# A descriptor ring of 32 KB, scans that write over their gathered rows, and two scans at other places in the order

## The chip, the core and the metric

The kernel runs on one core of a Trainium2 chip. The metric is the device time of one launch in microseconds (us). A core has five engines with queues of their own: PE (matrix products), DVE (vector work and scans along a row), ACT (functions by table), POOL (here: indirect DMAs, which gather or scatter rows by a list of indices) and SP (here: all other DMAs). Engines wait for one another and for DMAs by semaphores. An indirect DMA is prepared by POOL itself: it writes descriptors, one for each row to be moved, into a ring in on-chip memory, from which 16 DMA engines take them.

## What is computed

A vision tower on 16 images of 56 x 56 positions with 64 channels: a gated 3 x 3 token stage, a class token put ahead of each image, a layer norm with a linear recurrence along the sequence, and a mixture of four experts whose gates come from graph attention. The part that the change touches is the graph attention, over 16,384 nodes and 262,144 edges:

```python
h = (x_flat @ W_gat).reshape(M, HEADS, NUM_EXPERTS)
a_src = (h * att_src).sum(-1); a_dst = (h * att_dst).sum(-1)
e = leaky_relu(a_src[src] + a_dst[dst], negative_slope=0.2)
e_max = segment_max(e, dst)
ee = exp(e - e_max[dst])
alpha = ee / (segment_sum(ee, dst)[dst] + 1e-16)
agg = segment_sum(h[src] * alpha[:, :, None], dst) + b_gat
```

## The kernel before

**Front.** Two lanes of 56 steps go through the token stage, the recurrence and the projection, in 64 turns (`TURNS`); each engine works on a different step in one turn. The steps write the table of node rows (24 floats: h, a_src, a_dst) to HBM. Beside turns 4 to 22 the edges are sorted by destination on DVE, PE and ACT, POOL searches the first edge of each node (L766, 128 gathers of 128 indices each) and scatters a_dst to the first edges (L773, 128 scatters; the last 10 come after the gathers of chunk 0).

**Gathers.** The edges lie sorted as 128 rows (partitions) of 2048 columns. POOL then gathers the source rows from the table, one column at a time: L796 runs 2048 times, each time 128 rows of 24 floats. They go in 17 chunks k: fifteen of 128 columns, one of 96, one of 32. Chunk k lands in `ring[k % 2]`, a tile in on-chip memory (not the descriptor ring). Every run of 128 has semaphores of its own, two that take turns in groups of four; ahead of each group POOL waits until the group two before it has landed (`gather_group`, L753).

**Scans.** When chunk k has landed, DVE runs scan k (L1606): a running maximum, and running sums of the weights and of the weighted rows, along each partition. It reads `ring[k % 2]` and writes into `res[k % 2]`; SP stores that to `partial` in HBM and loads the a_dst of chunk k+2 (`scan_moves`, L554). POOL begins chunk k >= 2 when scan k-2 is done (`scan_used`, L793); scan k waits for the store of chunk k-2 (L1649).

**Order.** All orders are written out by hand. `SCAN_AFTER_TURN` puts scans 0 to 6 behind turns of the front, on DVE, ACT (its exponentials) and SP (its store) alike; `SCAN_AFTER_PAIR` puts scans 7 to 11 behind pairs of 512-node expert blocks, which follow the front; the others come after the last pair.

**Tail.** After the last store POOL joins the segments across partitions (L800, L803) and gathers the last edge row of each node (L811, 128 gathers); DVE, ACT and PE mix the experts' outputs and the result is stored. Ahead of that SP loads the table rows of the nodes themselves into the free half of `ring` (L657).

Of the kernel before, what the change touches and what calls it, by code (L numbers as in the profile page):

```python
# [5 lines left out]
i32 = mybir.dt.int32  # L6
bf16 = mybir.dt.bfloat16
# [26 lines left out]
P = 128  # L34
# [58 lines left out]
SC = 128  # L93
# [31 lines left out]
SCAN_AFTER_TURN = {31: 0, 37: 1, 43: 2, 49: 3, 55: 4, 61: 5, 63: 6}  # L125
# [21 lines left out]
def build(nc, x, cls_tok, tokW1, tokb1, tokW2, tokb2, tokW3, tokb3, A_diag, Bmat, Cmat, Dvec, dtv,  # L147
# [12 lines left out]
    with ctx:  # L160
# [48 lines left out]
        ring_all = sb("ring", [P, 2 * SC * TW])  # L209
        ring = [ring_all[:, n * SC * TW:(n + 1) * SC * TW].rearrange("p (a b) -> p a b", b=TW) for n in range(2)]  # L210
        res = [sb(f"res{n}", [P, SC, RW]) for n in range(2)]
        raw = [sb(f"raw{n}", [P, SC, HEADS]) for n in range(2)]
        ad = sb("ad", [P, HEADS, SC])
        e = sb("e", [P, HEADS, SC])
        mx = sb("mx", [P, HEADS, SC + 1])
# [19 lines left out]
        keys = [t[:, :, :].rearrange("p a b -> p (a b)")[:, 0:COLS] for t in res]  # L235
        dst_in = ns[:, :].bitcast(i32)
        dst_i = ring_all[:, 2 * COLS:3 * COLS].bitcast(i32)
        dst_f = keys[0]
        own_a = res[0][:, :, :].rearrange("p a b -> p (a b)")[:, COLS:COLS + P * HEADS].rearrange("p (a b) -> p a b", b=HEADS)
# [3 lines left out]
        iota_wide = ring_all[:, 2 * COLS:2 * COLS + SB * P // 2].bitcast(bf16).rearrange("p (a b) -> p a b", b=SB)  # L243
# [189 lines left out]
        def _(sp):  # L433
# [120 lines left out]
            def scan_moves(k):  # L554

                sp.wait_ge(S["scan_used"], k + 1)
                d(partial_v[:, FROM[k] * RW:(FROM[k] + SIZES[k]) * RW],
                  res[k % 2][:, 0:SIZES[k], :].rearrange("p a b -> p (a b)")).then_inc(res_st[k % 2], 16)
                if k + 2 < SCHUNKS:
                    load_raw(k + 2)  # L560
# [94 lines left out]
            for k in range(max(SCAN_AFTER_PAIR.values()) + 1, SCHUNKS - 1):  # L655
                scan_moves(k)
            d(own.rearrange("p (m j) w -> p m (j w)", j=FF), table[0:GRAPH_NODES, :]  # L657
# [20 lines left out]
        def _(pool):  # L678
# [106 lines left out]
            for k in range(SCHUNKS):  # L785
# [6 lines left out]
                if k >= 2:  # L792
                    pool.wait_ge(S["scan_used"], k - 1)  # L793
# [469 lines left out]
        def _(dve):  # L1263
# [342 lines left out]
            def scan(k):  # L1606
# [6 lines left out]
                ov = res[q][:, 0:n, :].rearrange("p c w -> p w c")  # L1613
# [35 lines left out]
                wait(dve, res_st[q], 16 * (k // 2))  # L1649
                v.tensor_copy(ov[:, 0:HEADS, :], mx_k)  # L1650
                for h in range(HEADS):
                    v.tensor_tensor_scan(ov[:, HEADS + h, :], old[:, h, :], new[:, h, :],
                                         car[:, HEADS + h:HEADS + h + 1], ALU.mult, ALU.add)
                    for x_ in range(EXPERTS):
                        w = h * EXPERTS + x_
                        v.tensor_tensor_scan(ov[:, 2 * HEADS + w, :], old[:, h, :], msg_k[:, w, :],
                                             car[:, 2 * HEADS + w:2 * HEADS + w + 1], ALU.mult, ALU.add)
                v.drain()
                v.tensor_copy(car[:, :], res[q][:, n - 1, :])
# [331 lines left out]
```

## Time and profile before

| | us |
|---|---|
| time, median of three runs (3934.3 to 3937.07) | 3935.76 |
| the profiled execution's own time | 3940.46 |
| its span, first to last instruction | 3938.5 |
| POOL busy | 2467.8 (63%) |
| DVE busy | 2236.6 (57%) |
| PE busy | 1959.2 (50%) |
| ACT busy | 1172.2 (30%) |
| gathers of L796: busy, idle ahead of them | 2023.7, 661.2 |

Shares of busy time are means over stages with different limits. To read them, take the stage apart in which one engine works without a break, and look at what ends each of its gaps. "issue" as the end of a gap says that the profile shows nothing that the engine waited for. The time of a POOL row for an indirect DMA is that of preparing it, not of moving the data.

### The profile page before, as it was taken

Reading aid. Unit: us, or ns where it says so; the run is one execution under the profiler, and the core shown is the slowest. Engines: PE = TensorE matmul, PEld = TensorE weight load, DVE = VectorE, ACT = ScalarE, POOL = GpSimd, SP = SyncE. Lnnn points to the kernel's source line nnn. Section 1 sums busy time; section 2 is a strip of 40 time slices with the busy share of each in tenths; the row PEclk is TensorE's granted clock in tenths of the full one; section 3 lists DMA queues with packets and bytes.
Section 4 is the critical chain, followed back from the end, with each engine's and each line's share of the span. In section 5 each row is a group of like instructions: output and inputs, shape, how many; then the busy total and the mean of one; then the engine's idle time right before and its main releaser. Section 6 shows DMA issues by size and latency. Waiting matters only on the chain. (4 is left out here: it accounts for less than half of the span.)

```text
span 3938.5 us, 28658 instructions
## 1 busy us (share of the span) xinstructions
PE 1959.2 (50%) x7633; PEld 850.9 (22%) x7633; DVE 2236.6 (57%) x3952; ACT 1172.2 (30%) x1736; POOL 2467.8 (63%) x2477
## 2 busy tenths in 40 slices
PE   0441119998876868686865036785863300000034
PEld 0111113333222323232322012332321100000023
DVE  8889987887567666767677555544322020210355
ACT  0120005554543434343433024553553300000000
POOL 1000007776777777777777777777777777777573
PEclk9975558998987989897977568997987755555567
DMA  4110004543443434444431433232332310111133
GB/s 110 26 26 0 0 11 76 100 77 69 76 70 77 78 73 75 83 71 77 81 60 27 78 51 78 67 86 69 86 112 52 111 28 10 28 10 27 39 116 127
DMA packets 651925, 247.81 MB, mean 63 GB/s; under 512 B 552260, under 2 KB 632564, under 8 KB 649332
## 3 DMA queue, kind: packets, MB, share of 16 engines
q1 hardware_dynamic: 573844, 216.69, 23.4%
q0 software_dynamic: 77920, 29.29, 7.2%
q8 instruction: 62, 1.02, 0.1%
q14 instruction: 99, 0.81, 0.1%
HBM read 152.62 MB, written 91.71 MB: 62 GB/s over the span
## 5 line engine op out<-in xcount | busy, mean ns | idle before, releaser
L796 POOL DMA_INDIRECT ring<-table,src_i x2048 | 2023.7, 988 | 661.2 <-issue 546.9
L766 POOL DMA_INDIRECT ring<-keys_d,place x128 | 147.7, 1154 | 627.6 <-DVEq L1269 587.5
L1625 DVE TENSOR_TENSOR_SCAN ad<-ns,cad,raw 128x128 f32<-128x128 f32 (+2 forms) x68 | 26.5, 451 | 745.6 <-DMA ring<-table,src_i 745.5
L1003 PE MATMUL ps<-arena 64*128 64x512 f32 x800 | 219.2, 670 | 396.8 <-DMA arena<-xnT 259.7
L898 PE MATMUL ps<-arena,w 64*128 64x448 f32 x896 | 255.4, 650 | 185.8 <-DVE arena L1668 114.6
L1050 PE MATMUL ps<-ident,ends 128*20 128x128 f32 x6 | 1.5, 414 | 596.3 <-DVEq L1865 596.3
L1123 ACT ACTIVATE ex<-ex 128x1024 f32<-128x1024 f32 (+2 forms) x17 | 17.1, 1006 | 831.0 <-DVE ex L1640 831.0
L1200 ACT ACTIVATE arena<-ps,arena 128x1024 f32<-128x1024 f32 x200 | 213.0, 1115 | 116.9 <-PE ps L1003 116.8
L1668 DVE TENSOR_TENSOR arena<-arena,ps 128x448 f32<-128x448 f32 x297 | 172.1, 616 | 115.5 <-ACT ps L1117 115.3
L911 PE MATMUL ps<-arena,w 128*64 128x448 f32 x896 | 216.5, 606 | 39.3 <-issue 39.3
L1117 ACT ACTIVATE ps<-ps,tb 128x448 f32<-128x448 f32 x297 | 169.6, 605 | 210.1 <-PE ps L898 190.2
L1682 DVE TENSOR_TENSOR_SCAN arena<-ps,carry,arena 128x448 f32<-128x448 f32 x122 | 130.7, 1131 | 163.2 <-ACT arena L1166 163.1
L1312 DVE TENSOR_TENSOR res<-res 128x512 f32<-128x512 f32 (+1 forms) x259 | 208.0, 803 | 13.2
L1836 DVE TENSOR_TENSOR arena<-ps,arena 128x1024 f32<-128x1024 f32 x68 | 83.3, 1225 | 221.1 <-PE ps L1025 220.6
L1313 DVE TENSOR_TENSOR res<-res 128x512 f32<-128x512 f32 (+1 forms) x259 | 206.5, 797 | 0.0
L1014 PE MATMUL ps<-arena 128*64 128x512 f32 x800 | 194.1, 606 | 0.0
L1003 PEld LDWEIGHTS ps<-arena 64*128 64x128 f32 x800 | 74.3, 201 | 534.4 <-issue 238.0
L888 PE MATMUL ps<-arena,w 128*64 128x448 f32 x896 | 186.6, 559 | 0.0
L773 POOL DMA_INDIRECT adst_d<-res,place x128 | 147.3, 1151 | 62.5 <-issue 38.2
L853 PE MATMUL ps<-ident,res 128*128 128x128 f32 x224 | 54.0, 422 | 243.2 <-DVE res L1335 193.2
L1207 ACT ACTIVATE arena<-ps,arena 128x512 f32<-128x512 f32 x200 | 126.6, 684 | 140.1 <-PE ps L1014 139.7
L1117 ACT ACTIVATE arena<-ps,tb 128x448 f32<-128x448 f32 x207 | 121.5, 631 | 128.9 <-PE ps L898 101.0
(346 smaller groups left out, 3952.1 us busy)
## 6 DMA issues: line engine op xcount, KB each, us to landing
arena<-in_x SPq DMA_DIRECT2D x304, 110.0 KB
ring<-table,src_i POOLq DMA_INDIRECT x2048
partial<-res SPq DMA_DIRECT2D x15, 1536.0 KB, 6.1
arena<-in_x SPq DMA_DIRECT2D x160, 140.0 KB
outputs_d<-arena SPq DMA_DIRECT2D x32, 512.0 KB, 2.8
arena<-outputs_d SPq DMA_DIRECT2D x32, 512.0 KB, 4.9
arena<-xnT SPq DMA_DIRECT2D x100, 128.0 KB, 3.1
arena<-h_tok SPq DMA_DIRECT2D x50, 256.0 KB
```

Of the source, the lines that this page charges most:

```text
L766: g.indirect_dma_start(out=blocks[:, k, :], out_offset=None, in_=keys_d[:, :], in_offset=off(ap=place[:, k:k + 1], axis=0)).then_inc(done, 16)
L796: g.indirect_dma_start(out=ring[k % 2][:, j - FROM[k], :], out_offset=None, in_=table[0:GRAPH_NODES, :], in_offset=off(ap=src_i[:, j:j + 1 ...
L888: mm(o[lower_upper(z), :], w1[:, i, :], tap_view(s, 2 * i + z), start=i == 0, stop=False, skip_group_check=True)
L898: mm(bank(1 + (2 * i + z) % 3)[:, 0:CHUNK], w2[lower_upper(z), i * P:(i + 1) * P], h1[lower_upper(z), :], start=True, stop=True).then_inc( ...
L911: mm(bank(4)[lower_upper(z), 0:CHUNK], w3[:, i, :], prod[:, 2 * i + z, :], start=i == 0, stop=False, skip_group_check=True)
L1003: m = mm(hid[ee % 2][:, z * NT:(z + 1) * NT], fw1[lower_upper(z), ee, :], xf[q][lower_upper(z), :], start=True, stop=True)
L1014: m = mm(sy[lower_upper(h), t * NT:(t + 1) * NT], fw2[:, ee, :], hh[k % 2][:, z, ee, :], start=True, stop=True)
L1117: a(gate_of(s, t), bank(1 + t % 3)[:, 0:CHUNK], ACT.Sigmoid, bias=tb2[:, t // 2:t // 2 + 1])\
L1200: a(hh[k % 2][:, :, ee, :], hid[ee % 2].rearrange("p (z n) -> p z n", z=2), ACT.Gelu, bias=fb1[:, ee:ee + 1]).then_inc(S["hh_done"], 1)
L1312: v.tensor_tensor(d4[:, :, 0:halves], low, high2, ALU.min)
L1313: v.tensor_tensor(d4[:, :, halves:size], high, low2, ALU.max)
L1668: v.tensor_tensor(r3(prod[:, t, :]), tap_view(s, t), r3(gate_of(s, t)), ALU.mult)\
```

## The change

1. The descriptor ring that POOL fills for its indirect DMAs has 32 KB in each partition, not 16 (`dynamic_dma_scratch_size`).
2. The tiles `res` are gone, which makes room for it. Scan k writes its results over the rows that it has read, in `ring[k % 2]`, and the store reads them there. The sort's key tiles, which lay in `res`, lie in an enlarged `ring`; some short-lived tiles moved into one new tile, `early_i`.
3. POOL therefore begins chunk k >= 2 when the store of chunk k-2 has landed (`res_st`), not when scan k-2 is done. Scan k no longer waits for a store. SP waits for the store of chunk 15 before it loads the nodes' own rows over that half.
4. Scan 4 stands behind turn 54, not 55, and scan 5 behind turn 59, not 61.

```diff
--- before.py
+++ after.py
@@ -122,7 +122,7 @@
 RAW_AT = 26
 PSUM_FROM = GRAPH_STEPS + 4
 EARLY_STEPS = 17
-SCAN_AFTER_TURN = {31: 0, 37: 1, 43: 2, 49: 3, 55: 4, 61: 5, 63: 6}
+SCAN_AFTER_TURN = {31: 0, 37: 1, 43: 2, 49: 3, 54: 4, 59: 5, 63: 6}
 SCAN_AFTER_PAIR = {4: 7, 14: 8, 24: 9, 35: 10, 44: 11}
 GROUP = 4
 
@@ -206,13 +206,15 @@
         ns = sb("ns", [P, COLS])
         src_i = sb("src_i", [P, COLS], i32)
 
-        ring_all = sb("ring", [P, 2 * SC * TW])
+        ring_all = sb("ring", [P, 2 * SC * TW + COLS])
         ring = [ring_all[:, n * SC * TW:(n + 1) * SC * TW].rearrange("p (a b) -> p a b", b=TW) for n in range(2)]
-        res = [sb(f"res{n}", [P, SC, RW]) for n in range(2)]
-        raw = [sb(f"raw{n}", [P, SC, HEADS]) for n in range(2)]
-        ad = sb("ad", [P, HEADS, SC])
+        assert RW == TW
+        HW = HEADS * SC
+        early_i = sb("early_i", [P, 3 * HW + HEADS * (SC + 1)])
+        raw = [early_i[:, n * HW:(n + 1) * HW].rearrange("p (a b) -> p a b", b=HEADS) for n in range(2)]
+        ad = early_i[:, 2 * HW:3 * HW].rearrange("p (a b) -> p a b", a=HEADS)
+        mx = early_i[:, 3 * HW:3 * HW + HEADS * (SC + 1)].rearrange("p (a b) -> p a b", a=HEADS)
         e = sb("e", [P, HEADS, SC])
-        mx = sb("mx", [P, HEADS, SC + 1])
         ex = sb("ex", [P, 2, HEADS, SC])
         msg = sb("msg", [P, HE, SC])
         nb = sb("nb", [P, SC])
@@ -232,15 +234,15 @@
         fixed = sb("fixed", [P, RW])
         none = sb("none", [1, RW])
 
-        keys = [t[:, :, :].rearrange("p a b -> p (a b)")[:, 0:COLS] for t in res]
+        keys = [ring_all[:, (2 + n) * COLS:(3 + n) * COLS] for n in range(2)]
         dst_in = ns[:, :].bitcast(i32)
-        dst_i = ring_all[:, 2 * COLS:3 * COLS].bitcast(i32)
+        dst_i = early_i[:, 0:COLS].bitcast(i32)
         dst_f = keys[0]
-        own_a = res[0][:, :, :].rearrange("p a b -> p (a b)")[:, COLS:COLS + P * HEADS].rearrange("p (a b) -> p a b", b=HEADS)
+        own_a = e[:, :, :].rearrange("p a b -> p (a b)").rearrange("p (a b) -> p a b", b=HEADS)
         SB = SAMPLES // 4
         oh = [[ring_all[:, n * SB * P // 2:(n + 1) * SB * P // 2].bitcast(bf16)
                .rearrange("p (a b) -> p a b", b=SB) for n in (2 * q, 2 * q + 1)] for q in range(2)]
-        iota_wide = ring_all[:, 2 * COLS:2 * COLS + SB * P // 2].bitcast(bf16).rearrange("p (a b) -> p a b", b=SB)
+        iota_wide = ex[:, :, :, :].rearrange("p z a b -> p (z a b)").bitcast(bf16).rearrange("p (a b) -> p a b", b=SB)
         blocks = ring_all[:, 0:P * SAMPLE].rearrange("p (a b) -> p a b", b=SAMPLE)
         rowbase = sb("rowbase", [P, 1])
 
@@ -555,7 +557,7 @@
 
                 sp.wait_ge(S["scan_used"], k + 1)
                 d(partial_v[:, FROM[k] * RW:(FROM[k] + SIZES[k]) * RW],
-                  res[k % 2][:, 0:SIZES[k], :].rearrange("p a b -> p (a b)")).then_inc(res_st[k % 2], 16)
+                  ring[k % 2][:, 0:SIZES[k], :].rearrange("p a b -> p (a b)")).then_inc(res_st[k % 2], 16)
                 if k + 2 < SCHUNKS:
                     load_raw(k + 2)
 
@@ -654,6 +656,7 @@
                 load_y(hidx)
             for k in range(max(SCAN_AFTER_PAIR.values()) + 1, SCHUNKS - 1):
                 scan_moves(k)
+            sp.wait_ge(res_st[1 - last_ring], 16 * len(SIZES[1 - last_ring::2]))
             d(own.rearrange("p (m j) w -> p m (j w)", j=FF), table[0:GRAPH_NODES, :]
               .rearrange("(m p j) w -> p m (j w)", p=P, j=FF)).then_inc(S["rows_in"], 16)
 
@@ -790,7 +793,7 @@
                             scatter(tile_k, group_landed(scattered, n))
                             n += 1
                 if k >= 2:
-                    pool.wait_ge(S["scan_used"], k - 1)
+                    pool.wait_ge(res_st[k % 2], 16 * (k // 2))
                 for j in range(FROM[k], FROM[k] + SIZES[k]):
                     done = gather_group(k, j - FROM[k])
                     g.indirect_dma_start(out=ring[k % 2][:, j - FROM[k], :], out_offset=None, in_=table[0:GRAPH_NODES, :],
@@ -1610,7 +1613,6 @@
                     dve.wait_ge(done, gathered(k) // 2)
                 dve.wait_ge(raws[q], 16 * (k // 2 + 1))
                 rv = ring[q][:, 0:n, :].rearrange("p c w -> p w c")
-                ov = res[q][:, 0:n, :].rearrange("p c w -> p w c")
                 cs = slice(FROM[k], FROM[k] + n)
 
                 flag = ns[:, cs].unsqueeze(1).broadcast_to([P, HEADS, n])
@@ -1646,17 +1648,16 @@
                                     new[:, h, :].unsqueeze(1).broadcast_to([P, EXPERTS, n]), ALU.mult)
                 v.drain()
 
-                wait(dve, res_st[q], 16 * (k // 2))
-                v.tensor_copy(ov[:, 0:HEADS, :], mx_k)
+                v.tensor_copy(rv[:, 0:HEADS, :], mx_k)
                 for h in range(HEADS):
-                    v.tensor_tensor_scan(ov[:, HEADS + h, :], old[:, h, :], new[:, h, :],
+                    v.tensor_tensor_scan(rv[:, HEADS + h, :], old[:, h, :], new[:, h, :],
                                          car[:, HEADS + h:HEADS + h + 1], ALU.mult, ALU.add)
                     for x_ in range(EXPERTS):
                         w = h * EXPERTS + x_
-                        v.tensor_tensor_scan(ov[:, 2 * HEADS + w, :], old[:, h, :], msg_k[:, w, :],
+                        v.tensor_tensor_scan(rv[:, 2 * HEADS + w, :], old[:, h, :], msg_k[:, w, :],
                                              car[:, 2 * HEADS + w:2 * HEADS + w + 1], ALU.mult, ALU.add)
                 v.drain()
-                v.tensor_copy(car[:, :], res[q][:, n - 1, :])
+                v.tensor_copy(car[:, :], ring[q][:, n - 1, :])
                 v.drain()
                 v.nop().then_inc(S["scan_used"], 1)
 
@@ -1981,7 +1982,8 @@
         "b1": np.ascontiguousarray(g["L0_ffn_b1"].T), "W2": g["L0_ffn_W2"], "b2": row(g["L0_ffn_b2"]),
         "edges": g["L0_ffn_edge_index"],
     }
-    nc = bacc.Bacc("TRN2", target_bir_lowering=False, num_devices=1)
+    nc = bacc.Bacc("TRN2", target_bir_lowering=False, num_devices=1,
+                   dynamic_dma_scratch_size=32768)
     args = [nc.dram_tensor("in_" + k, a.shape, mybir.dt.from_np(a.dtype), kind="ExternalInput").ap()
             for k, a in arrays.items()]
     args.append(nc.dram_tensor("out", [NODES, CH], f32, kind="ExternalOutput").ap())
```

How this moves instructions is seen at two places. The first is DVE at the front's end, just ahead of scan 6 (whose first row here is L1625, or L1627 in the changed kernel). `ad` and `early_i` are the a_dst along the columns, `carry` is the state of the recurrence. Before:

```order
L1656 SCALAR_TENSOR_TENSOR res<-ex,car,msg 128x128 x4
L1659 COPY car<-res 128x24
L1718 SCALAR_TENSOR_TENSOR arena<-arena,d_sb,ps 128x448
L1721 TENSOR_TENSOR arena<-arena 128x448
L1748 TENSOR_TENSOR arena<-ps,arena 128x448
L1625 SCALAR_TENSOR_TENSOR ad<-ns,cad,raw 128x128 x4
L1626 TENSOR_SCALAR nb<-ns 128x128
L1627 COPY mx<-car 128x4
```

The same place in the changed kernel:

```order
L1765 TENSOR_TENSOR arena<-arena 128x448 x2
L1769 COPY carry<-arena 128x1 x2
L1719 SCALAR_TENSOR_TENSOR arena<-arena,d_sb,ps 128x448
L1722 TENSOR_TENSOR arena<-arena 128x448
L1749 TENSOR_TENSOR arena<-ps,arena 128x448
L1627 SCALAR_TENSOR_TENSOR early_i<-ns,cad,early_i 128x128 x4
L1628 TENSOR_SCALAR nb<-ns 128x128
L1629 COPY early_i<-car 128x4
```

The end of scan 5 (the rows that write `car`) is no longer ahead of scan 6: it went in front of turns 60 and 61, and the end of turn 61 (`carry`) stands there now.

The second is SP at the end, where it stores the last chunks and loads the nodes' own rows (`ring<-table`). In brackets is what an issue waits for. Before:

```order
L552 DMA raw<-adst_d 128x384
L557 DMA partial<-res 128x3072 [waits scan_used]
L552 DMA raw<-adst_d 128x128
L557 DMA partial<-res 128x2304 [waits scan_used]
L657 DMA ring<-table 128x32x96
L557 DMA partial<-res 128x768 [waits scan_used]
```

In the changed kernel:

```order
L554 DMA early_i<-adst_d 128x384
L559 DMA partial<-ring 128x3072 [waits scan_used]
L554 DMA early_i<-adst_d 128x128
L559 DMA partial<-ring 128x2304 [waits scan_used]
L660 DMA ring<-table 128x32x96 [waits res_st1]
L559 DMA partial<-ring 128x768 [waits scan_used]
```

The order is the same; the load now waits for the store ahead of it.

## Rows read from the trace of the kernel before

**Rows 1.** Busy time by stretch: L796 alone; then all engines, PE to POOL.

```profile
990.90:3688.40 2697.50, 2023.70 (x2048) 0.76 0.32 64
...
3688.40:3938.50 250.10, 85.41 (x330) 69.23 (x330) 121.34 (x282) 20.44 (x56) 135.74 (x130) 0.68 0.33 99
```

**Rows 2.** Groups by line: busy, mean ns, idle ahead, and its releasers.

```profile
L796 POOL DMA_INDIRECT ring<-table,src_i x2048 | 2023.7, 988 | 661.2 <-issue 546.9 <-DMA ring<-table,src_i 114.3
```

**Rows 3.** Waits of POOL: total us, times, longest us; whole run, then chunk 15.

```profile
POOL ring L796 <- issue: 546.9, 1697, 3.2
POOL ring L796 <- DMA ring<-table,src_i: 114.3, 351, 2.1
...
POOL ring L796 <- issue: 22.5, 74, 0.3
```

**Rows 4.** Timeline of POOL at three pauses: start, us, gather [idle before it].

```profile
1140.56 0.94 POOL L796 DMA_INDIRECT ring<-table,src_i  x1 [3.13 <-issue]
...
3171.57 0.94 POOL L796 DMA_INDIRECT ring<-table,src_i  x1 [0.30 <-issue]
3174.49 0.94 POOL L796 DMA_INDIRECT ring<-table,src_i  x1 [1.97 <-issue]
...
3503.78 0.94 POOL L796 DMA_INDIRECT ring<-table,src_i  x1 [2.01 <-issue]
```

**Rows 5.** Gathers from the first of chunks 0 and 12 to its pause.

```profile
L796 POOL DMA_INDIRECT ring<-table,src_i x113 | 112.3, 994 | 34.4 <-issue 29.9 <-DMA ring<-table,src_i 4.6
...
L796 POOL DMA_INDIRECT ring<-table,src_i x113 | 110.1, 974 | 34.9 <-issue 27.9 <-DMA ring<-table,src_i 7.0
```

**Rows 6.** Timeline: the start of scan 12 on DVE, and a gather beside it.

```profile
3194.43 1.61 DVE L1625 TENSOR_TENSOR_SCAN ad<-ns,cad,raw 128x128 f32<-128x128 f32 x4 [141.93 <-DMA ring<-table,src_i]
...
3204.00 2.01 POOL L796 DMA_INDIRECT ring<-table,src_i  x1 [0.30 <-issue]
```

**Rows 7.** SP issues the stores of chunks 3, 4, 5; landing of all 17.

```profile
1810.44 0.33 SPq L557 DMA_DIRECT2D partial<-res  x1
...
2001.24 0.32 SPq L557 DMA_DIRECT2D partial<-res  x1
...
2170.12 0.32 SPq L557 DMA_DIRECT2D partial<-res  x1
...
DMA to landing us min/median/max: 2.3/6.1/6.6
```

**Rows 8.** The first gathers of chunks 5, 6 and 7.

```profile
1845.91 0.94 POOL L796 DMA_INDIRECT ring<-table,src_i  x1 [0.30 <-issue]
...
2015.04 0.94 POOL L796 DMA_INDIRECT ring<-table,src_i  x1 [0.30 <-issue]
...
2183.56 0.94 POOL L796 DMA_INDIRECT ring<-table,src_i  x1 [0.30 <-issue]
```

**Rows 9.** DVE: ends of turns 54 and 59; starts of scans 4, 5, 6.

```profile
1950.17 0.21 DVE L1768 COPY carry<-arena 128x1 f32<-128x1 f32 x2
...
1977.57 1.61 DVE L1625 TENSOR_TENSOR_SCAN ad<-ns,cad,raw 128x128 f32<-128x128 f32 x4
...
2111.29 0.21 DVE L1768 COPY carry<-arena 128x1 f32<-128x1 f32 x2
...
2146.45 1.61 DVE L1625 TENSOR_TENSOR_SCAN ad<-ns,cad,raw 128x128 f32<-128x128 f32 x4
...
2185.02 1.61 DVE L1625 TENSOR_TENSOR_SCAN ad<-ns,cad,raw 128x128 f32<-128x128 f32 x4 [6.99 <-DMA ring<-table,src_i]
```

**Rows 10.** The load of own rows on SP, and its first reader on DVE.

```profile
L657 SPq DMA_DIRECT2D ring<-table x1: 773/773/773, 3666.7 to 3666.7; - x1
DMA to landing us min/median/max: 11.7/11.7/11.7
...
3709.91 0.69 DVE L1905 TENSOR_TENSOR arena<-ring 128x512 f32<-128x512 f32 x1
```

**Rows 11.** DVE waits for the last search reads.

```profile
790.71 0.69 DVE L1559 TENSOR_TENSOR ring<-ring,msg 128x512 f32<-128x512 f32 x1 [1.05 <-DMA ring<-keys_d,place]
```

## The prediction

> **What bounds the kernel now.** I read first the busy time by stretch. All 2048 gathers of L796 lie in one stretch of 2697.5 us out of 3938.5; what follows is a tail of 250.1 us that works on their result [rows 1]. Within the stretch POOL is busy for 2023.7 us and idle for 661.2 us in gaps so short that no other engine can be blamed: 1697 gaps count as "issue" and 351 as waits for a gather's landing [rows 2, 3]. So the end of the program is the start of chunk 0 (991 us), plus 2048 gathers one behind the other, plus the tail; DVE does not hold POOL anywhere in it, and a scan is waited for only at the very end. A change is worth what it takes from POOL's row of gathers.
>
> Then I looked for gaps that are not like the others. An ordinary gap is 0.30 us. Chunk 15, which is 96 gathers, has 74 issue gaps of 22.5 us in total, 0.304 us each, the longest 0.3 [rows 3]. Over the whole loop the longest is 3.2 us [rows 3], and the timeline shows where the long ones lie: one in each of chunks 0 to 14, 15 in all, between 1.78 and 3.19 us; the first (3.13), that of chunk 12 (1.97) and the last (2.01) are shown [rows 4]. Their sum is 33.5 us, and 33.5 - 15 x 0.304 = **28.9 us** is more than ordinary gaps would take. The total agrees: 546.9 - 1697 x 0.304 = 31.0 us of issue time above the ordinary, so some 2 us lie elsewhere.
>
> The place of the pause is what matters. In chunk 0 and in chunk 12 alike, 113 gathers go out from the chunk's first one and the pause stands ahead of the 114th [rows 5]; the other 13 are 128 gathers apart. Between chunks 0 and 1 POOL also issues ten scatters, and the pause of chunk 1 is still ahead of the 114th gather of its chunk. So something fills up that is empty again at the start of each run of 128, and holds 113 DMAs. Chunks 15 and 16 have fewer than 113 columns and show no such pause. That is the size that the change doubles, as I read it: twice 113 is 226, and no run is longer than 128.
>
> **The change part by part.**
>
> The ring. 15 pauses go, if the count of 113 is the ring's: -28.9 us on POOL's row, at full price, since the next gather waits for nothing else there. What could be late next is the group wait ahead of every fourth gather; its 351 gaps are 114.3 us in total, 0.33 us each [rows 3], so groups have mostly landed by then, and I add nothing. The search and the scatters have a pause at their 114th DMA too, of about 1.4 us above the ordinary each. The scatter's is hidden: the step behind it waits for the front. The search's is waited for by DVE, 1.05 us [rows 11], and the front that sets the start of chunk 0 is behind DVE; between 0 and 1.05, and I take -1 us since nothing else is late there.
>
> Stores in place of scans, as what opens a chunk. POOL begins chunk k+2 at the landing of store k. A store lands 6.1 us after its issue, 6.6 at most [rows 7]. Without pauses (28.9 / 15 = 1.93 us each, and 1 us from the search) chunk 5 would start at 1845.9 - 5 x 1.93 - 1 = 1835.2 [rows 8]; store 3 goes out at 1810.4 [rows 7] and is down by 1817.0: 18 us of cover. Chunk 6 would start at 2015.0 - 12.6 = 2002.4; store 4 goes out at 2001.2 and, left where it is, would be down by 2007.8, 5 us late. Chunk 7 would start at 2183.6 - 14.5 = 2169.1; store 5 (2170.1 + 6.6 = 2176.7) would be 8 us late. Later scans start soon after their chunk has landed (scan 12 as shown [rows 6]) and take 23.7 us (scan 4: 1977.6 to its store at 2001.2 [rows 7, 9]), while the next chunk of 128 takes some 165: over 100 us of cover, and 98 for the chunk of 96. Price with the moves: 0. Behind the waiting gather on POOL there are only more gathers; nobody else waits for them before the chunk is full.
>
> The moves. Turn 55 lasts from 1950.2 to 1977.6 on DVE, so scan 4 and its store come 27.3 us sooner; turns 60 and 61 last from 2111.3 to 2146.5, so scan 5 comes 35 us sooner [rows 9]. Store 4 is then down by 1980, 22 us ahead of chunk 6; store 5 by 2142, 27 us ahead of chunk 7. Both scans find their chunk landed: the next chunks began at 1845.9 and 2015.0 [rows 8]. On SP the store and the load of a_dst for the chunk after next move along, past the x loads and step stores of one and two turns, and SP stands at the same wait for the scan, only sooner; the front's work of turns 55, 60 and 61 runs up to a scan's length (23.7 us) later, and nothing on POOL waits for it. Scan 6 waited 7.0 us for its chunk [rows 9] and still does, about 14 us sooner, and the expert pairs start as much sooner. Price: 0.
>
> Writing over the gathered rows. The operations of a scan keep their number, shape and stride (24 floats, in `res` as in `ring`); the one wait that goes (for a store two chunks back) had long been met. The nearest rows are those same instructions, so 0 either way; the sort's keys in another tile likewise.
>
> The nodes' own rows. Their load now starts when store 15 is down, about 4.6 us later than it did; it takes 11.7 us from 3666.7, and DVE reads it at 3709.9 [rows 10]. 31.5 us of cover less 4.6: 27 us. Behind it on SP is only the last store, which waits for scan 16. It no longer shares the DMA engines with store 15; the longest wait of a gather for a landing is 2.1 us [rows 3], so -1 to +2 us, and I take 0.
>
> Sum: -28.9 - 1 = about -30 us. The tail begins as much sooner and is unchanged. Made against the profiled execution: 3938.5 - 30 = 3908.5 of span; with 2 us around it 3910.5, against 3940.5. The median of the timed runs is 4.7 us below the profiled one, so 3935.8 - 30 = **3906 us**.
>
> **The rivals.**
>
> A, fewer pauses but not none. If the count runs on through the runs, one comes every 226 gathers: 2048 / 226 = 9 stay, 9 x 1.93 = 17.4 us, and the gain is 28.9 - 17.4 + 1 = 12.5: 3923. Against it: ten scatters between chunks 0 and 1 did not shift the place, and the later pauses lie 128 apart, not 113. The Trainium skill gives this case its mechanism: by "DMA: Bandwidth & Descriptors" (Terms, and The descriptor swizzle) a descriptor is 16 bytes and 128 rows make nine of them on each DMA engine, and by "SBUF — State Buffer" (SBUF size) the ring has 16 KiB per partition; an estimate from these pages is 1024 / 9 = 113.8 DMAs per round of the ring, wherever a run begins. The trace agrees with the 113 and not with rounds that run on.
>
> B, nothing, because the pause isn't the ring's. A mechanism of that kind is at work here: a gather beside scan 12 took 2.01 us to prepare where 0.94 is ordinary [rows 6], so DVE's work does slow POOL. If it also made the pauses, the ring would change nothing: 3935. Against it: at 3172.5 to 3174.5 DVE has been idle since scan 11, for 141.9 us up to scan 12 [rows 6], and the pause is there as in the other chunks. The Trainium skill has this as a rule: "SBUF — State Buffer", SBUF: two separate sides, says that POOL cannot write descriptors while DVE holds a port that they share. By that rule the time would stay at 3935; the trace agrees on the slowed gathers and not on the pauses.
>
> C, slower: POOL held at the stores. Place: the starts of chunks 5, 6 and 7, where the front is closest behind. The covers are 18, 22 and 27 us; it decides from there, if the front in its new order (or slower scans in place) runs that much later against the gathers, and each us more costs one. To lose on the whole it must eat the 30 us gained and 8 more, so a front some 60 us late by then, and a time above 3944. For it: without the moves two of the three would have been late. Against it: the front has the same work, of which a scan is 23.7 us.
>
> D, more than that: group waits and slowed gathers give up a little as well; 3897 at the best.
>
> **How the numbers follow.** Forecast 0.77, A 0.08, B 0.07, C 0.05, D 0.03. About 0.2% (8 us) is what a measurement can tell from no change. Faster by more: 0.77 + 0.08 + 0.03 = 0.88; within: B, 0.07; slower: C, 0.05. The forecast alone spans 3900 to 3912 (the unknown 0 to 1 of the search, -1 to +2 at the own rows, and gathers that fall otherwise beside DVE's work, some us either way). The range takes in A and most of D: 3898 to 3924, and leaves out B and C, 0.12, and a little of D.
>
> **What would show it.** In the profile after: no issue gap of L796 over 1 us; issue time about 517 us; last gather ending near 3658, the tail again 250 us. No wait of POOL for a `partial` store at a chunk's start (C shows there). Store 4 issued near 1973, store 5 near 2135. Pauses ahead of other gathers, at 226 or so, say A; at the 114th still, B. Wrong altogether I would be if the pauses only moved to the chunk starts.

## The result, and the profile after

The changed kernel takes **3911.0 us** (median of 6 runs, 3902.1 to 3913.4) against 3937.1 of the kernel before beside it (6 runs): a ratio of **0.9929, 95% interval 0.9916 to 0.9941**, 26 us less. The forecast was 3906, 30 us less, in a range of 3898 to 3924. The profiled execution took 3913.4 us, 27.1 us less than that of before; its span is 3911.4.

Busy time by stretch in the changed kernel (start:end, length, busy us of PE, PEld, DVE, ACT and POOL with their instruction counts, granted clock, DMA share, GB/s): up to the first gather, the gathers, the tail. It answers to [rows 1].

```profile
0.00:990.60 990.60, 502.89 (x1901) 224.71 (x1903) 839.53 (x1394) 276.23 (x440) 298.16 (x290) 0.78 0.26 50
990.60:3659.70 2669.10, 1368.56 (x5404) 554.05 (x5400) 1276.47 (x2278) 874.02 (x1240) 2027.13 (x2058) 0.76 0.33 65
3659.70:3911.40 251.70, 86.36 (x330) 69.91 (x330) 121.53 (x282) 20.40 (x56) 136.42 (x130) 0.68 0.33 98
```

The gather stretch is 28.3 us shorter (2669.1 against 2697.4 from first start to last end), it begins 0.5 us sooner, and the tail is 1.6 us longer, inside the 249.6 to 252.3 us that the tail took in the twelve kernels below. Then the gathers by line, and what POOL waited for (total us, times, longest us), as in [rows 2, 3]:

```profile
L799 POOL DMA_INDIRECT ring<-table,src_i x2048 | 2017.4, 985 | 639.2 <-issue 525.7 <-DMA ring<-table,src_i 113.6
```

```profile
POOL ring L799 <- issue: 525.7, 1706, 1.8
POOL ring L799 <- DMA ring<-table,src_i: 113.6, 342, 2.3
```

The issue time fell by 21.2 us, where the forecast of 517 wanted 30; the gathers themselves are 6.3 us less busy, which no step foresaw. The timeline of POOL around the 114th gather of chunk 0, and then at the first gathers of chunks 2, 4, 5 and 6 (start, us, gather, idle before it), shows both halves:

```profile
1134.94 0.94 POOL L799 DMA_INDIRECT ring<-table,src_i  x1 [0.30 <-issue]
1136.19 0.94 POOL L799 DMA_INDIRECT ring<-table,src_i  x1 [0.30 <-issue]
1137.44 0.94 POOL L799 DMA_INDIRECT ring<-table,src_i  x1 [0.30 <-DMA ring<-table,src_i]
...
1338.04 0.94 POOL L799 DMA_INDIRECT ring<-table,src_i  x1 [1.84 <-issue]
...
1670.79 0.94 POOL L799 DMA_INDIRECT ring<-table,src_i  x1 [1.32 <-issue]
...
1838.30 0.94 POOL L799 DMA_INDIRECT ring<-table,src_i  x1 [1.37 <-issue]
...
2003.03 0.94 POOL L799 DMA_INDIRECT ring<-table,src_i  x1 [0.30 <-issue]
```

At 1136.19, the 114th of chunk 0, stood 3.13 us of idle time before [rows 4]; now 0.30, and so in all 15 chunks. But the first gathers of chunks 2, 4 and 5 have new gaps, 3.6 us above ordinary ones (4.53 - 3 x 0.304), and in the other chunks' first gathers there is none. So there was something left to explain: the forecast had the ring never full, and so nothing at the chunk starts.

### The profile page after: what moved, and what is told of

Same layout as the page of the kernel before. It is cut to its first block and busy times, and to the rows that moved or that the text cites. A ratio compares the mean times of both kernels' runs of the same rounds, so it can differ in the third digit from the quotient of the medians.

```text
span 3911.4 us, 28658 instructions
## 1 busy us (share of the span) xinstructions
PE 1957.8 (50%) x7633; PEld 848.7 (22%) x7633; DVE 2237.5 (57%) x3952; ACT 1170.6 (30%) x1736; POOL 2461.7 (63%) x2477
## 5 line engine op out<-in xcount | busy, mean ns | idle before, releaser
L799 POOL DMA_INDIRECT ring<-table,src_i x2048 | 2017.4, 985 | 639.2 <-issue 525.7
L1627 DVE TENSOR_TENSOR_SCAN early_i<-ns,cad,early_i 128x128 f32<-128x128 f32 (+2 forms) x68 | 26.4, 450 | 719.0 <-DMA ring<-table,src_i 719.0
L1315 DVE TENSOR_TENSOR ring<-ring 128x512 f32<-128x512 f32 (+1 forms) x259 | 208.1, 804 | 13.2
L1316 DVE TENSOR_TENSOR ring<-ring 128x512 f32<-128x512 f32 (+1 forms) x259 | 206.8, 799 | 0.0
L776 POOL DMA_INDIRECT adst_d<-e,place x128 | 147.9, 1156 | 62.5 <-issue 48.5
L856 PE MATMUL ps<-ident,ring 128*128 128x128 f32 x224 | 54.0, 422 | 243.4 <-DVE ring L1338 193.3
L814 POOL DMA_INDIRECT ring<-partial,ends_i x128 | 134.1, 1048 | 40.1 <-issue 31.4
```

Source lines behind the costliest of these rows:

```text
L776: g.indirect_dma_start(out=adst_d, out_offset=off(ap=place[:, k:k + 1], axis=0), in_=own_a[:, k, :], in_offset=None).then_inc(done, 16)
L799: g.indirect_dma_start(out=ring[k % 2][:, j - FROM[k], :], out_offset=None, in_=table[0:GRAPH_NODES, :], in_offset=off(ap=src_i[:, j:j + 1 ...
L1315: v.tensor_tensor(d4[:, :, 0:halves], low, high2, ALU.min)
L1316: v.tensor_tensor(d4[:, :, halves:size], high, low2, ALU.max)
```

## The experiments

Two theories stood against each other once the changed kernel was seen. **Theory 1**, the prediction's: a chunk's 128 gathers overfill a ring that holds 113 DMAs, each filling costs 1.93 us, and a ring that holds more than 128 has none. **Theory 2**: a full ring costs by *which* gather's landing POOL then has to wait for, and that hangs on where in its group of four (the gathers that share a semaphore) the gather stands. The runs came in three batches, on two chips (one for e1 to e4 and e9 to e12, one for e5 to e8). The kernel before took 3955.7 us beside e1 to e4, 3940.9 beside e5 to e8 and 3952.0 beside e9 to e12; all ratios are to the kernel before in the same batch. "Loop" is the stretch of 2048 gathers in the profiled execution.

| run | ring, groups, kernel | ratio (95% interval) | loop, us | pauses at the ring's count or at a chunk's start, us above ordinary gaps |
|---|---|---|---|---|
| before | 16 KB, 4 | 1 | 2697.4 | 15, ahead of the 114th: 28.9 |
| after | 32 KB, 4 | 0.9929 (0.9916 to 0.9941) | 2669.1 | 3 chunk starts: 3.6 |
| e1 | 16 KB, 4, after | 0.9984 (0.9975 to 0.9994) | 2694.2 | 15, ahead of the 114th: 30.1 |
| e2 | 12 KB, 4, after | 0.9973 (0.9962 to 0.9985) | 2689.6 | 16, ahead of the 86th: 22.8 |
| e3 | 8 KB, 4, after | 0.9905 (0.9886 to 0.9923) | 2671.8 | 57th: one of 1.2; 109th: one of 2.2 |
| e4 | 32 KB, 4, after, no moves | 0.9914 (0.9892 to 0.9935) | 2682.7 | 3 chunk starts: 5.4 |
| e5 | 8 KB, 4, before | 0.9927 (0.9914 to 0.9939) | 2675.4 | 57th: one of 3.1 |
| e6 | 15 KB, 4, before | 0.9955 (0.9937 to 0.9972) | 2674.0 | 14, ahead of the 107th: 9.6 |
| e7 | 32 KB, 4, after again | 0.9929 (0.9916 to 0.9943) | 2670.5 | 3 chunk starts: 3.1 |
| e8 | 8 KB, 8, after | 0.9892 (0.9877 to 0.9906) | 2659.2 | none |
| e9 | 16 KB, 4 shifted, before | 0.9919 (0.9906 to 0.9933) | 2672.2 | 4, ahead of the 114th: 5.4 |
| e10 | 8 KB, 8, before | 0.9891 (0.9876 to 0.9906) | 2662.4 | none (one wait for a scan: 2.3) |
| e11 | 20 KB, 4, after | a single run, 3916.1 us | 2673.1 | 3 chunk starts: 3.8 |
| e12 | 32 KB, 8, after | 0.9886 (0.9870 to 0.9901) | 2669.5 | none |

**The ring's size alone: e1, e2, e3.** Three runs of the changed kernel with another number in its last statement (the diff is that of e1; 12288 in e2, 8192 in e3):

```diff
-                   dynamic_dma_scratch_size=32768)
+                   dynamic_dma_scratch_size=16384)
```

e1:

> The changed kernel with the ring alone put back to 16 KB; scans in place, waits for stores and the two moves stay. Theory (the ring makes the pauses): an issue gap of 1.8 to 3.2 us stands again ahead of the 114th gather of chunks 0 to 14, 28.9 us above ordinary gaps; the three smaller gaps that the changed kernel shows ahead of the first gather of chunks 2, 4 and 5 (1.84, 1.32 and 1.37 us) go. The gather loop is about 2695 us, the time about 3936. Rival (the gain comes from the other edits: gathers are 6.3 us less busy in the changed kernel, and the scans write elsewhere): the time stays at 3911, or half of the gain stays, 3925.

e2:

> The changed kernel with a ring of 12 KB. 113 DMAs at 16 KB make 84 or 85 at 12 KB. Both theories see one pause of some 2 us ahead of the 85th or 86th gather of chunks 0 to 15 (chunk 15 has 96 gathers): 16 pauses, about 31 us above ordinary gaps, 3938 to 3942. Rival (113 is no count of the ring): pauses elsewhere, or none, 3911.

e3:

> The changed kernel with a ring of 8 KB, which holds 56 DMAs. Theory 1 (every filling of the ring costs the same 1.93 us): pauses ahead of the 57th gather and of one near the 112th in chunks 0 to 14, one in chunk 15: 31 pauses, 60 us above ordinary gaps, about 3971. Theory 2 (a full ring waits for the newest DMA of which the semaphores of the groups of four can tell; ahead of the 114th, the second of a group, that is the one two back, whose landing comes 2.1 us before the pause ends): the 57th and the 109th are the first of a group, where the gathers five back have landed some 3 us before, so the full ring finds room at once: no pauses, or few of 1 to 1.8 us as at three chunk starts of the changed kernel, 3908 to 3920.

With 16 KB the 15 pauses are back at their place, 1.65 to 3.98 us each, and the gaps at the chunk starts are gone. POOL's issue time in e1, and its 114th gather of chunk 12:

```profile
POOL ring L799 <- issue: 548.6, 1700, 4.0
...
3171.28 0.94 POOL L799 DMA_INDIRECT ring<-table,src_i  x1 [2.03 <-issue]
```

The ratio of 0.9984 (0.9975 to 0.9994) leaves some 6 us to the other edits; e5 beside e7 below shows no such difference, and which is right stays open. With 12 KB the count is 85: POOL's gathers of chunk 12 from the first one, and the timeline at the 86th:

```profile
L799 POOL DMA_INDIRECT ring<-table,src_i x85 | 83.6, 984 | 26.2 <-issue 21.9 <-DMA ring<-table,src_i 4.3
...
3124.76 0.95 POOL L799 DMA_INDIRECT ring<-table,src_i  x1 [0.30 <-issue]
3127.36 0.94 POOL L799 DMA_INDIRECT ring<-table,src_i  x1 [1.64 <-issue]
```

So the count is the ring's, 85 : 113 as 12 : 16. (By the Trainium skill, "DMA: Bandwidth & Descriptors", The descriptor swizzle, a transfer to 128 partitions gives each DMA engine nine descriptors to read and nine to write; with the 16 bytes of a descriptor (the same page, Terms), 12288 / 16 / 9 = 85.3 is an estimate from that page. The trace agrees with 85.) The expected price was too high by 8 us: 22.8 us for 16 pauses, 1.43 each.

8 KB decides between the two. By the counts so far the ring holds 56, and each chunk fills it sooner and more than once, but there is no row of pauses. POOL in e3, the groups by line, and the timeline at the 57th gather of chunk 12:

```profile
L799 POOL DMA_INDIRECT ring<-table,src_i x2048 | 2020.1, 986 | 639.2 <-issue 525.3 <-DMA ring<-table,src_i 113.9
...
3079.17 0.95 POOL L799 DMA_INDIRECT ring<-table,src_i  x1 [0.30 <-issue]
3080.42 0.94 POOL L799 DMA_INDIRECT ring<-table,src_i  x1 [0.30 <-issue]
```

3080.42 is the 57th (the chunk begins at 3006.81): 0.30 us. The idle time of the whole loop, 639.2 us, is that of the changed kernel with a ring four times as large. Theory 1, which had 3971 here, falls; a smaller ring can do what the larger one does. Of the 31 gaps ahead of a chunk's 57th and 109th gather two are longer than 0.5 us, 1.54 and 2.49.

**The moves: e4.**

```diff
-SCAN_AFTER_TURN = {31: 0, 37: 1, 43: 2, 49: 3, 54: 4, 59: 5, 63: 6}
+SCAN_AFTER_TURN = {31: 0, 37: 1, 43: 2, 49: 3, 55: 4, 61: 5, 63: 6}
```

> The changed kernel with scans 4 and 5 put back behind turns 55 and 61. Theory (the moves keep POOL from being held at a store): store 4 goes out near 2001 us and is down near 2007.5, where POOL could open chunk 6 at 2003.0, and store 5 near 2170 (down 2176.5), where POOL, already 4.5 us late, could open chunk 7 at 2173.3: POOL waits for a partial store at both places, 4.5 and 3 us, 7 to 8 us in all, time about 3918. Rival (the stores come early enough anyway): no wait of POOL for a store, 3911.

The store of chunk 4 and its landing in e4, and POOL at the first gather of chunk 6:

```profile
2000.01 0.32 SPq L559 DMA_DIRECT2D partial<-ring  x1
...
DMA to landing us min/median/max: 6.3/6.3/6.3
...
2007.46 0.95 POOL L799 DMA_INDIRECT ring<-table,src_i  x1 [0.30 <-DMA ring<-table,src_i]
2012.44 0.94 POOL L799 DMA_INDIRECT ring<-table,src_i  x1 [4.04 <-issue]
```

There is a gap of 4.0 us at chunk 6, but the store was down at 2006.3, 2.1 us before POOL had prepared the last gather of chunk 5 (2008.4), and the profile names no store. At chunk 7 there is none: store 5 goes out at 2168.3, and POOL, slower in this execution, ends chunk 6 only at 2181. The ratio, 0.9914 (0.9892 to 0.9935), has the 0.9929 of the kernel with the moves inside its interval, but that was measured elsewhere. So the moves can't be told from nothing here, where 7 to 8 us were expected of them, and whether the 4.0 us are the store's or one of the chunk-start gaps is not settled.

**The kernel before with a smaller ring: e5 and e6.** One number each, everything else as before (the diff is that of e5; 15360 in e6):

```diff
-    nc = bacc.Bacc("TRN2", target_bir_lowering=False, num_devices=1)
+    nc = bacc.Bacc("TRN2", target_bir_lowering=False, num_devices=1, dynamic_dma_scratch_size=8192)
```

e5:

> The kernel before with one edit: its ring is 8 KB, not 16. Nothing else changes: result tiles, waits for scans and turns are those of before. Theory 2 (a full ring costs by the DMA that it waits for; at 8 KB the waits fall on the first gather of a group, where that DMA is five back): no pause ahead of the 57th, 109th or 114th gather, loop near 2671 us, 26 us less than before, ratio 0.993 to 0.994. Of that up to 1 us may be given back at chunk 7, where scan 5 ends (2170.1) about when POOL gets there (2169). Rival (a smaller ring costs more, and the 8 KB run with the other edits was fast because of these edits): 31 pauses, 3965 or so where before takes 3936, ratio 1.007.

e6:

> The kernel before with a ring of 15 KB, one edit. It holds 106 DMAs, so it is full ahead of the 107th gather of a chunk, the third of its group of four. Theory 2: the DMA waited for is three back, which has landed some 1.37 us before the gather ahead is prepared; the pauses ended 2.13 us after that landing at 113 DMAs and 1.77 us at 85, so some 2.05 us at 106: gaps of about 0.7 us, 0.4 us above ordinary ones, in chunks 0 to 14 (more in the front, where landings are late), some 6 to 9 us in all; time about 20 us below before, ratio 0.995. Theory 1 (each filling costs 1.93 us): 15 pauses of 1.9 us and more, no change, ratio 1.000.

e7, the changed kernel beside them:

> The changed kernel as it is, on the chip of the other three, as their yardstick: ratio 0.993, and again gaps of 1 to 2 us ahead of the first gather of some of chunks 1 to 6 (three of them, 3.6 us above ordinary gaps, in its first profile), which the kernels with 8, 12 and 16 KB did not show. Rival: those gaps were chance and come at other places.

Halving the ring of the kernel before gives 0.9927, doubling it with all that it takes in the tiles gives 0.9929 on the same chip. In e7 the chunk-start gaps stand at chunks 3, 4 and 8, not at 2, 4 and 5: that there are some came again, at which chunks did not. POOL's waits in e5:

```profile
POOL ring L796 <- issue: 527.0, 1709, 3.4
POOL ring L796 <- DMA ring<-table,src_i: 110.8, 339, 1.9
```

The issue time is within 2 us of the changed kernel's 525.7. With 15 KB the count is 106, the 107th is the third of its group, and the pauses are there but small. Chunk 12 in e6, its 106 gathers and the 107th:

```profile
L796 POOL DMA_INDIRECT ring<-table,src_i x106 | 103.5, 976 | 32.5 <-issue 26.8 <-DMA ring<-table,src_i 5.8
...
3137.83 0.94 POOL L796 DMA_INDIRECT ring<-table,src_i  x1 [0.30 <-issue]
3139.30 0.94 POOL L796 DMA_INDIRECT ring<-table,src_i  x1 [0.53 <-issue]
```

0.53 us where 16 KB had 1.97 [rows 4]. Over the 15 chunks the sum is 9.6 us where 6 to 9 were expected; the ratio of 0.9955 where 0.995 was.

The landings say why. A gather's landing is not a row of the views, but its packets are in the trace. This is the share of the DMA engines in the kernel before from 3169 to 3175 us, in 40 slices of 0.15 us, around the pause of chunk 12 that ends at 3174.49 [rows 4]:

```profile
DMA  0008100000033000000430000000410000000000
```

Four gathers pass; the last two, prepared from 3170.33 and 3171.57, move their rows up to 3172.1 and 3173.5 in this row, and their last packets, too small to show in it, end at 3172.4 and 3173.5. The pause ends 2.1 us after the one and 0.9 after the other. Which of the two it waits for is seen where the front's transfers delay them. Time from the last packet of the gather one, two, three or five back to the start of the gather that paused, median (least to most):

| kernel | count, place in group | one back | two back | three back | five back |
|---|---|---|---|---|---|
| before, 16 KB | 113, second | 0.86 (0.25 to 1.93) | **2.12 (2.07 to 2.93)** | 3.35 (3.24 to 4.43) | |
| e1, 16 KB | 113, second | 0.88 (0.47 to 2.03) | **2.14 (2.10 to 2.96)** | 3.40 (2.77 to 5.37) | |
| e2, 12 KB | 85, second | 0.48 (0.04 to 1.31) | **1.78 (1.72 to 2.68)** | 3.05 (2.65 to 4.00) | |
| e6, 15 KB | 106, third | -0.48 (-1.70 to 1.17) | 0.77 (0.09 to 2.23) | **2.03 (1.98 to 2.75)** | |
| e9, 16 KB shifted, its four pauses | 113, first | | 1.37 (-0.38 to 2.11) | | **4.26 (4.16 to 4.67)** |

In the first four rows one column has a sharp least value, with most of the pauses within 0.1 us of it: the last gather of the group before. For the second of a group that is the one two back, for the third the one three back. That POOL must learn of it from the semaphore that the group shares is my inference; the numbers are the trace's. It takes POOL a fixed time more after that landing, 1.78 us with 85 DMAs in the ring, 2.03 with 106, 2.12 with 113. The row of e9, for the first of a group, says less: it has four pauses, and a gather ahead of which there is no gap also starts some 4.2 us after the landing of the one five back (the other eleven chunks of e9: median 4.18). What it does show is that neither the gather one back nor the one two back is waited for, since pauses end as much as 1.2 and 0.4 us before these have landed. With the ring not full, a late landing five back holds POOL only until 1.1 to 2.4 us after it (the group waits below); in these four it is 4.2 to 4.7.

**The place in the group alone: e9.** The kernel before, its ring of 16 KB untouched; only the groups are cut three places sooner:

```diff
-                half = i // GROUP % 2
-                if i % GROUP == 0 and i >= 2 * GROUP:
-                    hold(gath[k % 2][half], (gathered(k) - 16 * SIZES[k]) // 2 + 16 * (i // GROUP // 2 * GROUP))
-                elif i % GROUP == 0 and k:
-                    hold(gath[1 - k % 2][half], gathered(k - 1) // 2)
+                m = (i + 3) // GROUP
+                half = m % 2
+                start = (gathered(k) - 16 * SIZES[k]) // 2
+                if (i + 3) % GROUP == 0 and m >= 2:
+                    hold(gath[k % 2][half], start + 16 * ((m // 2 * GROUP) - 3 * (1 - half)))
+                elif i == 0 and k:
+                    hold(gath[1 - k % 2][0], gathered(k - 1) // 2 - 48)
+                elif i == 1 and k:
+                    hold(gath[1 - k % 2][1], gathered(k - 1) // 2)
```

> The kernel before with its ring of 16 KB, and one edit: the groups of four gathers on a semaphore begin three places sooner, so that the first group of each chunk has one gather and the last three; the 114th gather of a chunk is now the first of its group instead of the second. At a chunk's first gather POOL then waits for the gather eight back, at the second for the one five back. Theory 2 (what a full ring costs hangs on which landing POOL can tell: for the first of a group one five back, some 3.9 us before): the ring is as full as before at the 114th gather, but no pause of 1.8 to 3.2 us stands there, or one only where landings in the front are late; loop near 2672, ratio 0.993. Rival (the ring's size sets the pauses, and groups have no part): 15 pauses, 28.9 us, ratio 1.000.

The ratio is 0.9919. In chunk 12 of e9, 113 gathers and then the 114th, which starts at 3149.95:

```profile
L800 POOL DMA_INDIRECT ring<-table,src_i x113 | 110.0, 974 | 34.7 <-issue 27.4 <-DMA ring<-table,src_i 7.3
...
3148.71 0.94 POOL L800 DMA_INDIRECT ring<-table,src_i  x1 [0.30 <-issue]
3149.95 0.94 POOL L800 DMA_INDIRECT ring<-table,src_i  x1 [0.30 <-issue]
```

In 11 of the 15 chunks the 114th has an ordinary gap; four have 0.7 to 3.5 us (chunks 2, 4, 8 and 10), 5.4 us above ordinary in all instead of 28.9. The same execution holds its own yardstick: the groups of the search and of the scatters were not shifted, and both keep the pause ahead of their 114th DMA (in this kernel the search is L770, the scatters L777, the gathers L800):

```profile
764.47 0.95 POOL L770 DMA_INDIRECT ring<-keys_d,place  x1 [1.73 <-issue]
...
979.80 0.97 POOL L777 DMA_INDIRECT adst_d<-res,place  x1 [1.67 <-issue]
```

The same ring, as full as it was, with most of the pauses gone where the groups were shifted and in place where they were not: that the cost hangs on the place in the group is shown, and neither the larger ring nor the room made for it is what the gain needs. By what means POOL comes to wait for just that landing is not shown.

**Groups of eight: e8, e10, e12, and the chunk starts: e11.**

```diff
-GROUP = 4
+GROUP = 8
```

The groups of the search, the scatters and the tail's gathers grow with it. e8 and e10 have this edit and the 8 KB, e12 this one alone; e11 is the changed kernel with 20480 for 32768.

e8, on the changed kernel with 8 KB:

> The changed kernel with a ring of 8 KB and groups of eight gathers, not four, on a semaphore. The waits of a group then look nine gathers back instead of five. Theory (the gaps of 0.8 to 2.5 us that are left in the loop, seven to eleven of them and 10 to 12 us above ordinary ones, end about 1.5 us after the landing of the gather five back, which was late there; nine back it has landed): most of these gaps go, the loop is 8 to 11 us shorter than that of 8 KB and groups of four (2671.8), the ratio about 0.990. Rival (late landings hold POOL through something else, the queue itself): the gaps stay, ratio as the changed kernel's.

e10, on the kernel before with 8 KB:

> The kernel before with two edits of a number: ring of 8 KB, groups of eight. Result tiles, waits for scans and turns are those of before. Theory (ring and groups carry the whole gain, scans in place and moves none): no gap over 0.7 us inside a chunk, ratio 0.989 as for the same two edits on the changed kernel (0.9892); but POOL now comes to chunks 5 to 7 some 10 us sooner against the front than in the kernel before with 8 KB alone, and scans 4 and 5, not moved, open chunks 6 and 7: POOL may be held there by 2 to 5 us each, ratio up to 0.991. Rival (place in the tiles matters): 0.993.

e12, on the changed kernel with 32 KB:

> The changed kernel, 32 KB, with groups of eight, one edit. Theory: the gaps at groups go as with 8 KB and groups of eight, so the ratio is 0.989 to 0.990; at a chunk's first gather the wait is now for a gather nine back, so the gaps there, 3 us in all, go too. Rival (what fills up at the chunk's start with 32 KB does not hang on the group): some gaps of 1 to 2 us stay at the first gathers, and nowhere else.

POOL's waits in e8, and its groups by line:

```profile
POOL ring L799 <- issue: 574.2, 1884, 0.3
POOL ring L799 <- DMA ring<-table,src_i: 50.0, 164, 0.3
...
L799 POOL DMA_INDIRECT ring<-table,src_i x2048 | 2022.6, 988 | 624.1 <-issue 574.2 <-DMA ring<-table,src_i 50.0
```

The longest wait in 2048 gathers is 0.3 us: nothing is left but ordinary gaps (2048 x 0.305 = 625). With groups of four each trace had 4 to 11 gaps of 0.7 to 3.8 us at the group waits. In the changed kernel there are 8, 10.8 us above ordinary. Seven of them end 1.1 to 2.4 us after a late landing of the gather five back; the eighth, ahead of the 29th gather of chunk 16, ends 4.6 us after it. Nine back, all had landed. e8, e10 and e12 stand at 0.989, the fastest of all; e8 is 13 us below the changed kernel on its chip (3898.8 against 3912.0). In e12 the loop of the profiled execution gained only some 1 us on e7, since its gathers were 11 us busier (2032.6 against 2021.5); its timed runs show the gain (0.9886 against 0.9929, though in another batch).

e10 needs two numbers changed in the kernel before. It shows the one place where the tiles and moves are seen to matter, chunk 7, whose ring waits there for scan 5:

```profile
2164.68 0.18 DVE L1659 COPY car<-res 128x24 f32<-128x24 f32 x1
...
2161.85 1.20 POOL L796 DMA_INDIRECT ring<-table,src_i  x1 [0.30 <-issue]
2165.66 0.94 POOL L796 DMA_INDIRECT ring<-table,src_i  x1 [2.62 <-DVEq L1660]
```

That is 2.3 us above an ordinary gap, the lower end of the 2 to 5 us expected; chunk 6 had none.

e11:

> The changed kernel with a ring of 20 KB, one look. By 113 DMAs at 16 KB and 85 at 12 KB it holds 142, more than a chunk has. If the gaps ahead of a chunk's first gather, which only the kernels with 32 KB show (3 of 16 chunks in each of three profiles, 1.1 to 4.0 us), come whenever a ring holds more than the 128 gathers of a chunk, some of them stand here too. If they belong to 32 KB alone, or were chance, none is here.

The gaps stand in e11 too, at chunks 3, 4 and 8 (1.27, 2.46 and 1.00 us), as at 2, 4, 5 after, 3, 4, 6 in e4 and 3, 4, 8 in e7, and at no chunk start of the rings of 16 KB and less but the one of e10 just shown. So they come with a ring that holds more than 128. In the changed kernel, e7 and e11 these gathers start 4.2 to 5.4 us after the landing of the gather five back, as the late ones of e9 do (4.2 to 4.7). That fits a ring that counts as full at 128 DMAs whatever its size, the first gather of a chunk being the first of a group. But what holds the 128 was not isolated, and the chunk's start is not the only place: the gap of 1.6 to 1.8 us ahead of the 29th gather of chunk 16, in the same four kernels, has the same sign (4.3 to 4.6 us), 124 gathers after the start of chunk 15.

## Why the prediction was right, and where it was not

**The amount was right, its cause half so.** The 15 pauses are the ring's (85 : 106 : 113 as 12 : 15 : 16 KB), stood at full price on POOL's row, and went: -28.9 us, as summed. The step "twice 113 is 226, and no run is longer than 128" held for the 114th gathers, and e1 shows that it is the ring that took the pauses away: with 16 KB they are back. As a reason it is too narrow: a ring of 56 DMAs does as well, and so, nearly, does one of 113 with the groups cut elsewhere. What failed is the premise beside it, that each filling costs the same (1.93 us, as rival A has it), and the sign "no issue gap of L796 over 1 us". The cost hangs on the landing waited for, two back at the second gather of a group, three at the third, with little or no pause at the first; and issue gaps of 1.3 to 1.8 us came at three chunk starts and ahead of the 29th gather of chunk 16. A row hinted at it: the pause stands at the 114th in every chunk, and 114 = 28 x 4 + 2. The only groups in the working were those of the group waits.

**The sum.** Gathers: -28.9 of pauses, +3.6 at the chunk starts, +3.4 at group waits (10.8 against 7.4), -6.3 of busy time, together -28.2, where -28.3 was measured. The forecast had the first alone, so that its nearness is in part luck: without the busy time the loop would have gained 22 us. "Wrong altogether I would be if the pauses only moved to the chunk starts" came true for an eighth of them. The busy time I take for chance: in the thirteen other traces it lies between 2020 and 2033 us, and it is 2021.5 for the same kernel again. It holds more than the pauses did: before, a gather takes 988 ns on average [rows 2] where the median is 945, some 88 us in all; 184 gathers take over 1.1 us, 110 of them beside a scan on DVE as in [rows 6]. So "DVE does not hold POOL anywhere in it" says more than the rows do; no run here tried to take this time away. With the start and the tail the profiled execution comes to -27.1, the medians to -26.1.

**The search.** Its pause went (DVE no longer waits 1.05 us for the last search reads [rows 11]), but the gathers began 0.5 us sooner, not 1: the load ahead of them waited 4.8 us for the front, 3.5 before, so the front is what is late next.

**Stores, moves, tiles, own rows: 0.** Stores 4 and 5 went out as forecast (1973 and 2135), 29 and 34 us ahead of the first gathers of chunks 6 and 7 (2003.0 and 2168.8), and scan 6 found its chunk landed:

```profile
1973.82 0.32 SPq L559 DMA_DIRECT2D partial<-ring  x1
...
2134.93 0.32 SPq L559 DMA_DIRECT2D partial<-ring  x1
...
2181.53 1.60 DVE L1627 TENSOR_TENSOR_SCAN early_i<-ns,cad,early_i 128x128 f32<-128x128 f32 x4
```

The forecast had scan 6 still waiting for its chunk, as in [rows 9]; it now starts without a wait, since the front is what is late there. The load of the own rows was issued at 3642.3 and down 8.8 us later; DVE read it at 3681.2, 30 us of cover. That tiles, store waits and moves together cost nothing is what e5 beside e7 (0.9927 and 0.9929) and e8 beside e10 (0.9892 and 0.9891) suggest, to some 5 us either way; in e1 they seem to gain 6. The tiles alone were not tried.

**The rivals.** A (a count that runs on) and B (DVE makes the pauses) fall with e2, e6 and e9: the place follows the ring and the groups. C did not come: in the changed kernel every store was down at least 21 us ahead of the chunk that it opens. Its place was well chosen all the same; in e10, where POOL comes to chunk 7 some 18 us sooner than before (2165.7 against 2183.6), the scan of chunk 5 holds it there for 2.3 us. D ("group waits give up a little") did not come either; in the changed kernel they took 3.4 us more than before. What there was to get was 10.8 us in 8 gaps, and with groups of eight they are gone.

## What to carry to other kernels

When a full queue stops an engine, ask which completion it must see before it goes on, not only how much the queue holds: here halving the ring, doubling it, or shifting the groups of four by three places gave much the same, 0.7 to 0.8%. So before room is cleared for a larger buffer, try to place the point where it fills behind work that is long done: here, with one semaphore per group, at the first transfer of a group. And a wait on the transfer five back that is met nearly always can still cost 10 us in a row of 2048; look at its longest waits, and look further back.

## What the runs showed of the hardware that I had not expected

- A smaller descriptor ring can be faster: 8 KB gave 0.9927 of the time with 16 KB, as 32 KB did (0.9929).
- A gather that finds the ring full at the second or third place of a group starts a nearly fixed time after the landing that it waits for, and that time grows with what is in the ring: 1.78 us at 85 DMAs, 2.03 at 106, 2.12 at 113, about 12 ns more for each DMA (0.34 / 28).
- The landing waited for is that of the last gather of the group before, and at the first of a group not that one, and by four pauses of e9 the one five back: pauses of 1.4 to 2.0 us above an ordinary gap on average at the second place, 0.6 at the third, few at the first.
- With rings of 20 and 32 KB some chunks' first gathers have gaps of 1.0 to 2.5 us (4.0 once), with 8 to 16 KB none had by itself; whether a ring that holds 142 or more counts as full at 128, and why every run of 128 begins anew at 16 KB, stays open.
